# Second cross attention: VectorE's order with independent operations between dependent ones, and the high part of the spread keys written by ScalarE

## The reference, cut to what matters

```
def _layernorm(x, axis=-1, eps=1e-05):
    m = jnp.mean(x, axis=axis, keepdims=True)
    v = jnp.var(x, axis=axis, keepdims=True)
    return (x - m) / jnp.sqrt(v + eps)
...
def _L1_xattn_ref(q, k, v, mask, w_q, w_k, w_v, w_o):
    ...
    query = proj(q, w_q)
    key_ = proj(k, w_k)
    value = proj(v, w_v)
    scores = jnp.einsum('bhqd,bhkd->bhqk', query, key_) / jnp.sqrt(jnp.asarray(D_K, dtype=query.dtype))
    scores = jnp.where(mask == 0, jnp.asarray(NEG, dtype=scores.dtype), scores)
    attn = jax.nn.softmax(scores, axis=-1)
    out = jnp.einsum('bhqk,bhkd->bhqd', attn, value)
    out = out.transpose(0, 2, 1, 3).reshape(B, -1, H * D_K)
    return out @ w_o.T
```

## Time and profile before

| what | value |
|---|---|
| median of 3 runs | 1612.04 us (1609.6 to 1612.83) |
| the profiled execution | 1622.13 us |
| its span, first to last instruction | 1619.9 us |
| mean granted TensorE clock over the span | 0.973 |

### The profile page before, as it was taken

The page is one execution under the profiler, slowest core; times in us unless marked ns, Lnnn a source line. Parts: engine busy times, 40 slices in busy tenths (PEclk is TensorE's granted clock), DMA queues, the critical chain, the costliest instruction groups (busy, mean ns, idle before and its releaser), DMA issues.

```text
span 1619.9 us, 37516 instructions
## 1 busy us (share of the span) xinstructions
PE 1460.8 (90%) x11740; PEld 1196.8 (74%) x11803; DVE 1229.3 (76%) x3032; ACT 1110.5 (69%) x2666; POOL 908.2 (56%) x789
## 2 busy tenths in 40 slices
PE   4899999999988998888887899999898899999988
PEld 3677777777766776666665788888776788888866
DVE  6888888888755556888886788888666787777765
ACT  4888778877754556777774787787723778778732
POOL 4667778777731113444433777777401777777500
PEclk9999999999998997999998999999999999999999
DMA  9800000000012321210000000000000000000000
GB/s 380 325 1 8 11 10 10 11 11 17 13 53 69 87 79 28 62 39 22 22 19 9 13 15 15 15 14 16 10 11 5 5 17 14 15 15 14 11 24 34
DMA packets 87336, 62.62 MB, mean 39 GB/s; under 512 B 52037, under 2 KB 72901, under 8 KB 86469
## 3 DMA queue, kind: packets, MB, share of 16 engines
q1 hardware_dynamic: 83141, 53.00, 10.5%
q0 software_dynamic: 4096, 8.40, 1.8%
HBM read 21.30 MB, written 30.41 MB: 32 GB/s over the span
## 4 chain that ended last, share of the span: by engine, by line
PE 53%; DVE 27%; ACT 9%; issue 6%; POOL 3%; DMA 1%; DVEq 0%; another core or an unknown queue 0%; SPq 0%; POOLq 0%; ACTq 0%
PE slot L1685 6%; PE slot L461 5%; PE slot L463 4%; PE slot L462 4%; PE slot L1668 4%; PE slot L1629 4%; PE slot L1703 3%; PE slot L1638 3%; ACT a_p L743 3%; DVE a_sum L861 3%; PE slot L1938 2%; POOL a_rq L1106 2%; DVE a_ssq L971 2%; PE slot L1679 2%; PE slot L1189 2%
## 5 line engine op out<-in xcount | busy, mean ns | idle before, releaser
L1045 POOL TENSOR_TENSOR rs<-mv,nhalf 128x1 f32 (+1 forms) x160 | 96.6, 604 | 240.2 <-DVE mv L1040 175.1
L1854 POOL TENSOR_TENSOR d_A<-d_A,d_B 128x1024 f32<-128x1024 f32 x64 | 150.8, 2356 | 134.0 <-DVE d_B L1792 133.8
L1858 POOL TENSOR_TENSOR d_r<-d_vv,nhalf 128x16 f32<-128x16 f32 x64 | 186.5, 2914 | 47.5 <-DVE d_vv L1814 46.9
L743 ACT ACTIVATE d_p<-slot,d_nm,d_r 128x128 f32<-128x128 f32 x512 | 185.6, 468 | 27.2 <-DVE d_nm L1805 27.2
L743 ACT ACTIVATE a_p<-slot,a_nm,a_rq 128x77 f32<-128x77 f32 x512 | 163.7, 432 | 56.5 <-DVE a_nm L768 56.5
L743 ACT ACTIVATE c_p<-slot,c_nm 128x77 f32<-128x77 f32 x512 | 116.9, 359 | 30.2 <-DVE c_nm L1477 30.2
L1685 PE MATMUL slot<-d_v,d_pT 128*128 128x65 f32 x1024 | 121.8, 272 | 1.7 <-ACT d_pT L1722 1.7
L1685 PEld LDWEIGHTS slot<-d_v,d_pT 128*128 128x128 f32 x1024 | 119.4, 192 | 2.4 <-ACT d_pT L1722 2.1
L750 POOL TENSOR_TENSOR a_p<-a_p,a_rc 128x616 f32<-128x616 f32 x64 | 80.0, 1250 | 71.5 <-DVE a_rc L863 70.9
L1773 DVE TENSOR_TENSOR d_A<-slot,T 128x1024 f32<-128x1024 f32 x64 | 78.3, 1224 | 45.6 <-PE slot L1629 45.5
L1801 DVE TENSOR_REDUCE slot<-slot 128x8 f32<-128x1024 f32 x64 | 78.9, 1233 | 28.1 <-PE slot L1668 25.5
(11 more groups left out here) (288 smaller groups left out, 4495.2 us busy)
## 6 DMA issues: line engine op xcount, KB each, us to landing
routed<-zero SPq DMA_DIRECT2D x2, 9216.0 KB, 48.6
b_x<-routed SPq DMA_DIRECT2D x80, 64.0 KB
answers<-b_y SPq DMA_DIRECT2D x40, 128.0 KB
X<-in_x SPq DMA_DIRECT2D x2, 1024.0 KB, 8.1
d_zx<-Z SPq DMA_DIRECT2D x64, 32.0 KB
H<-Z SPq DMA_DIRECT2D x64, 32.0 KB
out<-f_o SPq DMA_DIRECT2D x8, 256.0 KB, 2.0
d_zx<-Z SPq DMA_DIRECT2D x64, 31.8 KB
```

The source lines that it names most:

```text
L743: i = e.activation(t["p"][:, h, :], R[slot][:, k // nbank, nk * (k % nbank):nk * (k % nbank) + nk], ACT.Exp, bias=t["nm"][:, h:h + 1], sca ...
L1045: return e.tensor_tensor(rs[:, bass.ds(b, 1)], mv[:, bass.ds(b, 1), 1:2].rearrange("p a b -> p (a b)"), nhalf[:, 0:1], ALU.pow)
L1854: e.tensor_tensor(t["A"][:, p, :], t["A"][:, p, :], t["B"][:, p, :], ALU.add).then_inc(S("d_key"), 1)
L1858: e.tensor_tensor(t["r"][:, it.m(2, 4), :], t["vv"][:, p, :], nhalf[:, 0:16], ALU.pow).then_inc(S("d_key"), 1)
```

## The change

On ScalarE four activations are added between `c_qTh` and `c_kh`: each reads the projected keys in PSUM, multiplies them by one column of `head` (a scale that is a pointer to a value for each partition), and writes one of the four copies of `c_kbh`. The VectorE instruction at L1515 that wrote all four copies is removed. On VectorE the rest of the step is put in another order, with the same operations: the three steps of statistics of batch i-1 stand between the low parts of batch i-3, and the residual addition and statistics of batch i-6 stand between the reciprocal, `c_oT` and `c_xT`.

```
                     e.activation(t["qT"][0][:, it.m(3, 2), :], R[0][:, 0, 0:128], ACT.Copy, scale=float(DH1) ** -0.5)
+                    for j in range(4):
+                        e.activation(t["kb"][0][:, it.m(3, 2), j, :], R[0][:, 0, 128:128 + SK], ACT.Copy, scale=head[:, j:j + 1])
                     e.activation(t["kh"][:], R[0][:, 0, 128:128 + SK], ACT.Copy)
...
-                    e.wait_ge(S("c_mix"), count(b, 2, 2))
-                    apart(e)
-                    e.bn_stats(st[:, 1, :], rows(X, b)).then_inc(S("c_st"), 1)
-                    e.wait_ge(S("c_st"), count(b, 1, 3))
-                    apart(e)
-                    e.bn_aggr(agg[:, 1, :], st[:, 1, :]).then_inc(S("c_st"), 1)
-                    e.wait_ge(S("c_st"), count(b, 2, 3))
-                    e.tensor_tensor(rows(mv, b), agg[:, 1:2, :], eps[:, 1:2, :], ALU.add).then_inc(S("c_st"), 1)
+                b1 = b
                 b = it.b(3)
                 if b is not None:
                     e.wait_ge(S("ac_v"), count(b, base=NB))
                     e.scalar_tensor_tensor(out=t["qT"][1][:, it.m(3, 2), :], in0=R[0][:, 0, 0:128], scalar=float(DH1) ** -0.5,
                                            in1=t["qT"][0][:, it.m(3, 2), :].bitcast(F32), op0=ALU.mult, op1=ALU.subtract)\
                         .then_inc(S("c_sp"), 1)
+                if b1 is not None:
+                    e.wait_ge(S("c_mix"), count(b1, 2, 2))
+                    apart(e)
+                    e.bn_stats(st[:, 1, :], rows(X, b1)).then_inc(S("c_st"), 1)
+                if b is not None:
                     e.tensor_tensor(t["kl"][:], R[0][:, 0, 128:128 + SK], t["kh"][:].bitcast(F32), ALU.subtract)\
                         .then_inc(S("c_sp"), 1)
+                if b1 is not None:
+                    e.wait_ge(S("c_st"), count(b1, 1, 3))
+                    apart(e)
+                    e.bn_aggr(agg[:, 1, :], st[:, 1, :]).then_inc(S("c_st"), 1)
+                if b is not None:
                     blocks = head[:].unsqueeze(2).to_broadcast([128, 4, SK])
-                    e.tensor_tensor(t["kb"][0][:, it.m(3, 2), :, :], t["kh"][:].bitcast(F32).unsqueeze(1).to_broadcast([128, 4, SK]),
-                                    blocks, ALU.mult)
                     e.wait_ge(S("c_sp"), count(b, 2, 3))
                     e.tensor_tensor(t["kb"][1][:, it.m(3, 2), :, :], t["kl"][:].unsqueeze(1).to_broadcast([128, 4, SK]),
                                     blocks, ALU.mult).then_inc(S("c_sp"), 1)
+                if b1 is not None:
+                    e.wait_ge(S("c_st"), count(b1, 2, 3))
+                    e.tensor_tensor(rows(mv, b1), agg[:, 1:2, :], eps[:, 1:2, :], ALU.add).then_inc(S("c_st"), 1)
...
+                if b4 is not None:
+                    e.tensor_tensor(rows(X, b4), rows(X, b4), R[0][:, 1:2, 256:384], ALU.add).then_inc(S("ac_add"), 1)
                 if b3 is not None:
                     e.wait_ge(S("ac_PV"), count(b3, base=NB))
                     e.reciprocal(t["rcT"][:], R[0][:, 1, 384:512]).then_inc(S("c_rcT"), 1)
+                if b4 is not None:
+                    e.wait_ge(S("ac_add"), count(b4, base=NB))
+                    apart(e)
+                    e.bn_stats(st[:, 0, :], rows(X, b4)).then_inc(S("ac_bn"), 1)
+                if b3 is not None:
                     e.wait_ge(S("c_rcT"), count(b3))
                     e.tensor_tensor(t["oT"][:, it.m(5, 2), :], R[0][:, 1, 0:128], t["rcT"][:], ALU.mult).then_inc(S("ac_oTe"), 1)
                 if b0 is not None:
                     e.wait_ge(S("ac_xTp"), count(b0, base=NB))
                     e.tensor_copy(t["xT"][:, it.m(2, 2), :], R[0][:, 1, 128:256]).then_inc(S("ac_xh"), 1)
                 if b4 is not None:
-                    e.tensor_tensor(rows(X, b4), rows(X, b4), R[0][:, 1:2, 256:384], ALU.add).then_inc(S("ac_add"), 1)
-                if b4 is not None:
-                    e.wait_ge(S("ac_add"), count(b4, base=NB))
-                    apart(e)
-                    e.bn_stats(st[:, 0, :], rows(X, b4)).then_inc(S("ac_bn"), 1)
                     stats_tail(e, b4, S("ac_bn"), S("ac_ag"), S("ac_ve"), base=NB)
```

## The result

The changed kernel takes 1620.1 us (median of 9 runs, 1615.1 to 1627.7), the kernel before 1609.6 in the same comparison. The ratio is 1.0066 with a 95% interval of 1.0047 to 1.0085: slower by some 10.5 us where +5 was forecast. A later comparison gave 1619.6 against 1607.7, ratio 1.0080 (1.0061 to 1.0099). The time lies in the forecast's range, on the forecast's side, and about twice as far out. The 1617.0 us of the forecast are missed by only 3.1 because its base, the median of three runs, was 2.4 us above the 1609.6 of nine.

The account below looks back on a forecast made before the run. Stage c's step was taken as bound by a loop of waits, no engine full. Per step +0.84 (copies) - 0.49 (tail) - 0.13 (r) = +0.22 us, over 22 steps about +5, on 1612.0 gives 1617.0 us; range 1608 to 1627.

Parts of the forecast that it names:

- the head: Stage c, from the start of half a's c_nm to c_qTl; ScalarE's way 3.23 us, four copies add 0.84.
- The tail: Stage c, VectorE from c_qTl to the next c_nm; from 3.94 + r to 3.45 + r, 0.49 us shorter.
- the hesitation r: VectorE's wait between c_kbl and the reciprocal, 0.28 us in the step read; 0.13 counted as gained, the rest kept.
- rival 1: Stage c: TensorE swallows the longer head, or gaps and head cancel, -0.04 us a step; 1611 to 1614 us; chance 0.22.
- The part of r called remote: Share of VectorE's wait before the reciprocal, 2.8 us over 26 steps, 0.11 each; forecast to stay.
- rival 5: TensorE idles some 0.2 us more a step and its granted clock falls more often: +9 on top, 1626; chance 0.09.
- ScalarE's own loop: Stage c, exponentials through half b's c_pT: ends at 8.28, next exponentials start at 8.65, so 0.37 us are left.
- Rival 2: ScalarE's pointer copies cost only 0.12 us each: -0.14 us a step, 1608.4 us; chance 0.14.
- Rival 4: VectorE's gaps are not filled, the tail is 0.35 us longer: +1.19 a step, 1638 us; chance 0.03.
- Rivals 1 and 3: Rival 1 as above; the third: ScalarE's copies cost 0.31 us each, +13.6 us, 1625.7 us; chance 0.06.

Follow-up runs that it names:

- e1: The changed kernel without the four ScalarE copies, the VectorE instruction kept: the new VectorE order alone; 1599.1 us, ratio 0.9931 to the kernel before.
- e2: The kernel before with the four ScalarE copies added and L1515 removed, VectorE in its old order; 1636.2 us, ratio 1.0157 to the kernel before.
- e6: The kernel before with mask products ahead of the wait for low spread keys and eight overwritten ones added per step; 1606.2 us, ratio 0.9974.
- e4: The changed kernel with mask products ahead of the wait for low spread keys and eight overwritten ones added per step; 1610.2 us, ratio 1.0007.
- e5: The changed kernel with its mask products ahead of the wait for the low spread keys, none added; 1618.2 us, ratio 1.0049 to the kernel before.
- e8: The changed kernel with the four copies behind the values, reading the high keys in SBUF, with their own semaphore; 1608.1 us, ratio 0.9981 to the kernel before.
- e3: The changed kernel with the four copies lacking their pointer scale, so no head mask multiplication; 1605.8 us, ratio 0.9967 to the kernel before.
- e10: The new VectorE order without ScalarE copies, mask products ahead of the wait and eight overwritten ones added per step; 1594.5 us, ratio 0.9914.

## Why it came out slower, and where the forecast was short

**The mechanism was right.** ScalarE's way through the head already ended last or level, the four copies cost 0.21 us each, and the head is 4.09 us for a forecast of 3.23 + 0.84 = 4.07. VectorE's removed instruction, its filled gaps and the three operations moved out of the head could not pay for it. e1 and e2 show both halves by themselves: the order alone gains 11 us, the copies alone lose 26, part of it beyond the length of the chains.

**The tail was sized too long.** Forecast 3.45 + 0.15, measured 3.30. Half of the 0.30 is the hesitation r, which vanished whole, as I had left to rival 1; the other half is hundredths in many distances, 0.05 of them at `bn_stats` in front of `c_oT` (0.15 instead of 0.20).

**The step to start from was wrong.** I took 7.60 us as the step of before at full clock. Four steps of its own profile take 7.22 to 7.25, and in e6 the plain step is 7.26. The part of r called remote, which I kept, went too. TensorE being late doesn't explain it: in the step of the earlier trace rows the output projection had ended at 730.59, two microseconds ahead of the reciprocal:

```profile
730.20 0.39 PE L1433 MATMUL slot<-l,c_oT 128*128 128x128 f32 x2
```

What that wait is stays open. With e6's step the change at full clock is 7.40 - 7.26 = +0.14 us, over 26 steps +3.6. The kernels with filler, whose clocks are nearly the same (0.983 and 0.985), differ by 1610.2 - 1606.2 = 4.0 us. I take that for the part of the loss that lies in the chains. It is near the forecast's 5 by luck: the tail 0.30 too long and the step of before 0.34 too long nearly cancel. The timed runs agree: those with a clock of 0.970 or 0.971 take 1616.8 us in the mean of four of the changed kernel and 1613.8 in the mean of six of before, 3.0 apart.

**The step that failed is the one that gave the clock to a rival.** The sum counted TensorE's longer wait as idle time that costs nothing, and held rival 5 for unlikely. TensorE's wait for `c_kbl` nearly doubled, the clock over the span fell from 0.976 to 0.968, and the remaining 10.5 - 4.0 = 6.5 us go with it. That the clock costs time here is shown: e4 fills the idle time with products nobody needs and gets 10 us back with the same plain step, and e5 without the filling doesn't. The size, 6.5 us, is a difference of medians and takes e6's shorter step for the step of before; against the 7.6 us of before's own profile the chains would have gained and the clock would owe more than the whole loss. Rival 5's price, +9 on top of the forecast's +5, was of the right order and too high.

**ScalarE's own loop** had 0.37 us of room by the forecast. In the changed kernel the second `c_pT` ends at 688.37 + 0.81 = 689.18 and the exponentials start at 689.29 when `c_nm` comes, so 0.1 is left. Both loops are near 7.4 us; e8 takes the copies out of the one and is held by the other.

**The other rivals.** Rival 2 did not occur, for the copies cost 0.21 us each. Its mechanism is confirmed by e3: at 0.12 a copy the kernel is faster, 1605.8 us for the 1608.4 given. Rival 4, the gaps that stay, is refuted by the timeline above and by e1. Rivals 1 and 3 did not occur.

**What stays open.** In every profile, e10's at full clock too, the tail is 0.2 to 0.3 us longer in the last third of the stage, and with it the plain step (7.66 to 7.7 in the changed kernel, 7.2 in e1) except in e8, where ScalarE's loop sets the step and the head shrinks instead. It was not looked into. What in TensorE's idle pattern makes the clock fall wasn't settled either: e3 has a plain step of 7.04 and still a clock of 0.973, and e8 has as much idle time in the stage as the changed kernel (30.8 us against 31.6), waits of up to 2.2 us for `c_pT`, and 0.979.

## What to carry to other kernels

Before an operation is given to another engine because that one is less busy, see who waits for the receiving engine's next signal: four cheap copies ahead of a semaphore lengthened that wait by their full 0.84 us. The reordering that came with them was worth 11 us by itself, so two edits with one aim are to be timed apart. And when an edit lengthens the waits of an engine with a gated clock, count the clock too: here, by the two kernels with filler, it cost more than the chain did, and harmless work in the gap bought it back.

## What the runs showed of the hardware

- An activation of 128 x 77 from PSUM costs 0.12 us from start to start with no pointer operand (e3), 0.21 with one, be it a scale of a copy or a bias of an exponential, and 0.31 with two. The Trainium skill, "ScalarE: Activation LUTs", "What ACT_TABLE_LOAD costs", gives 93 ns for a pointer operand, and the trace agrees (0.09 to 0.10). By its figures the spacing with one pointer is an estimated 186 + 0.833 x 77 + 93 - 93 = 250 ns, 0.04 us more than the 0.21 measured here.
- The granted clock falls to its lower level although TensorE never waits long: the longest wait for the low spread keys in the changed kernel's stage is 1.9 us, and TensorE is busy 85% of the stage. With the gaps filled the stage's clock is 0.97 (e4, 14.4 us idle) or 1.00 (e6, 7.9; e10, 3.6). Between unfilled kernels the sum of the idle time does not order it: 28.2 us idle at 0.82 in e2, 29.7 at 0.94 before, 30.8 at 0.96 in e8, 31.6 at 0.92 in the changed kernel.
- Vector operations that depend on the one in front start 0.15 us after its end. With others between them that time is used, and a satisfied wait with its extra semaphore instruction costs nothing that shows: `bn_stats` behind the reciprocal starts at 687.39, 0.08 us before that has ended.
